# Message tiles of a two-layer graph network: a PSUM ring of eight tiles instead of four, and VectorE's loops written out

## The chip, the cores and the metric

One core of a Trainium2 chip runs the whole program. The metric is the device time of one execution in microseconds (us), lower is better. The engines are TensorE (PE, with its weight loads as PEld), VectorE (DVE), ScalarE (ACT), GpSimd (POOL) and SyncE (SP). PSUM has eight banks of 512 float32 values per partition; a message tile (128 edges by 256 features in float32) takes half a bank.

## The reference

```python
h = jnp.maximum(_layernorm(x), 0.0)                       # x: 3125 x 256
support = h @ L0_weight
msgs = support[src] * edge_weight[:, None]                # 50000 edges
x = x + segment_sum(msgs, dst, 3125) + L0_bias
h = jnp.maximum(_layernorm(x), 0.0)
xt = einsum('ni,rio->rno', h, L1_weight)                  # 8 relations
messages = xt[edge_type, dst]
x = x + relu(segment_sum(messages, src, 3125) + L1_bias)
```

Both layers gather one row of 256 values per edge from a table in DRAM and add it to the row of its target node. Layer 0 adds by `dst`, layer 1 by `src`.

## The kernel before

The edges are taken in four chunks of 25,000: chunks 1 and 2 (`m` = 0, 1) are the halves of layer 0, chunks 3 and 4 (`m` = 2, 3) those of layer 1. Each chunk is sorted by target block of 128 nodes into `T` = 220 tiles of 128 places, in groups of `U` = 20 tiles (eleven groups per chunk). For each tile four engines work in turn:

- POOL issues an indirect gather of 128 rows into a ring in SBUF (L440 in layer 0, ring of 20 tiles, one gather per tile; L456 in layer 1, ring of 32, 196 gathers per chunk). In layer 0 the indices of four gathers at a time are copied by ACT (`refill`, L535) after the message that last used the slots.
- DVE writes the one-hot matrix `oh_m` of the tile's target rows five tiles ahead (`one_hot`, L910, L913).
- PE multiplies it with the gathered rows into half a PSUM bank (`message`, L1304, and `step_message`, L1323).
- DVE adds that half bank to the block's rows four tiles later (`accumulate`, L925), at an offset that it loads into registers four tiles at a time (`offsets`, L917).

Message tiles take turns in banks 2 and 3: a ring of `RING` = 4 tiles. PE may write an even tile `t` only when tile `t` - 3 has been added (a wait on `s_acc`, one per pair of tiles); DVE adds a pair when both of its messages are there (a wait on `s_msg`).

While a chunk's messages run, the next chunk is sorted in the same instruction streams. Every five tiles DVE makes one block of one-hots (`sort_fields`, L848, in layer 0 also L852 and L853), ACT scales it (L502, fifteen instructions per block for the second chunk, ten for the later ones), DVE writes one `oh_t` per tile (L860), and PE runs two to five matmuls per tile (`sort_column`, L1295). In chunks 1 and 2 the chunk after next is ranked too: in groups 0 to 4 PE counts blocks from DVE's masks (L674), group 5 (`chain_side`) is a serial chain between DVE and PE (`rank_chain`; waits at L744, L773), and groups 6 to 9 take places (`take_places`, L707, from PE's matmuls L1243 and L1245). In the last group DVE decodes the sorted index of the next chunk (L868 to L903). During chunk 2 PE also makes layer 1's table (L1440) in banks 4, 5 and 6.

Every engine runs its instructions in the order in which they are written. PE's code is written out tile by tile. DVE's is written out for chunks 2 and 4; for chunks 1 and 3 (`phase`) groups 1 to 4 are one loop (L1017), groups 6 to 9 another (L1021), with addresses and wait values worked out in registers; groups 0, 5 and 10 are written out.

Of the kernel before, what the change touches and what calls it, by code (L numbers as in the profile page):

```python
# [5 lines left out]
def gnn_kernel(nc, x, src, dst, etype, ew, w0, b0, w1, b1, out):  # L6
# [4 lines left out]
    ALU = mybir.AluOpType  # L11
    ACT = mybir.ActivationFunctionType
    ds = bass.ds

    P = 128
    N, D = x.shape
# [11 lines left out]
    NS = 2 * CH  # L28

    T = (EP * CC + (P - 1) * NB) // P  # L30
    U = 20
# [7 lines left out]
    OR = 10  # L39
    RF = 4  # L40
    RING = 4

    BEHIND = (0, 8, 3, 3)
    TU = 5
    SI = CC // U
# [52 lines left out]
    with ctx:  # L98
        def sb(name, shape, dt=f32):
            return ctx.enter_context(nc.sbuf_tensor(name, shape, dt))  # L100
# [3 lines left out]
        def sb_under(name, shape, dt=f32):  # L104
            at[name] = -(-nc.sbuf_base // 32) * 32
            return sb(name, shape, dt)
# [4 lines left out]
        def sem(name):  # L111
            return ctx.enter_context(nc.semaphore(name))
# [47 lines left out]
                      for j, n in enumerate(("hi", "lo")))  # L160
# [50 lines left out]
        rows = sb_under("rows", [P, U, D])  # L211
# [16 lines left out]
        oh_m = sb("oh_m", [P, OR, P])  # L228
        oh_f0 = [sb_over("w1_hi" if k < 3 else "w1_sb", f"oh_f0_{k}", [EP, FR, P, G], f16 if k < 2 else bf16,
                         off=k % 3 * FR * P * G * 2) for k in range(5)]  # L230
# [9 lines left out]
        bank = [ctx.enter_context(nc.psum_tensor(f"bank{i}", [P, 512], f32)) for i in range(8)]  # L240
# [38 lines left out]
        def column(k):  # L279
            return RANK[0:KP, 320 + k:321 + k]  # L280

        def message_bank(u):
            return bank[2 + u // 2 % 2][:, u % 2 * D:(u % 2 + 1) * D]

        s_const = sem("s_const")
        s_ident = sem("s_ident")
# [65 lines left out]
        s_acc = sem("s_acc")  # L352
# [267 lines left out]
        def _(dve):  # L620
# [7 lines left out]
            V = nc.vector  # L628
# [20 lines left out]
            def buckets(s):  # L649
                node = dst_i if s < CH else src_i  # L650
                step(V.tensor_scalar(tmp_i[:, :], chunk(node, s), 7, None, ALU.logical_shift_right))
                step(V.tensor_copy(bucket[:, :], tmp_i[:, :]))
# [191 lines left out]
            def sort_fields(s, c, group, r):  # L844

                places, into = ring_of(s)
                dve.wait_ge(s_sortfree, c + (G + col0(s)))
                V.tensor_tensor(places[:, r, :, :], iota_g16[0:EP, :, :], over_places(pos_p[s % 2], c),  # L848
                                ALU.is_equal).then_inc(s_ohp, 1)
                if s < CH:  # L850
                    dve.wait_ge(s_ohp, group + (col0(s) // G + 1))
                    V.tensor_tensor(into[0][:, r, :, :], places[:, r, :, :], over_places(hi16[s], c), ALU.mult)  # L852
                    V.tensor_tensor(into[1][:, r, :, :], places[:, r, :, :], over_places(lo16[s], c), ALU.mult)  # L853
                if s == 0:
                    V.tensor_tensor(into[2][:, r, :, :], places[:, r, :, :], over_places(ew16[0], c), ALU.mult)
                    if c >= MORE:
                        V.tensor_tensor(into[3][:, r, :, :], places[:, r, :, :], over_places(ew16[1], c), ALU.mult)

            def sort_tile(s, c, slot):
                V.tensor_scalar(oh_t[:, slot, :], iota_t16[0:EP, :], pos_t[s % 2][:, ds(c, 1)], None,  # L860
                                ALU.is_equal).then_inc(s_sortready, 1)
# [46 lines left out]
            def one_hot(s, t, slot):  # L908
                if s < CH:
                    V.tensor_scalar(oh_m[:, slot, :], iota_p[:, :], local[s % 2][:, ds(t, 1)],  # L910
                                    ew_s[s % 2][:, ds(t, 1)], ALU.is_equal, ALU.mult).then_inc(s_ohm, 1)
                else:
                    V.tensor_scalar(oh_m[:, slot, :], iota_p[:, :], local[s % 2][:, ds(t, 1)], None,  # L913
                                    ALU.is_equal).then_inc(s_ohm, 1)

            def offsets(s, t):
                _, got = nc.values_load_multi_w_load_instructions(  # L917
                    tile_off[s % (NS - 1)][0:1, ds(t, LAG)], engines=[mybir.EngineType.DVE], min_val=0,
                    max_val=(NB - 1) * D, skip_runtime_bounds_check_because="tile_offsets() clamps them")
                return got  # L920

            def accumulate(s, off, u, t):
                acc = (x1_sb if s < CH else agg1)[:, :, :].rearrange("p b d -> p (b d)")
                dve.wait_ge(s_acc, t + (s * T + 1))
                V.tensor_tensor(acc[:, ds(off, D)], acc[:, ds(off, D)], message_bank(u), ALU.add).then_inc(s_acc, 1)  # L925

            def message_group(m, i, first=False, last=False, sort=False, side=None, summed=None, after=None):

                for u in range(U):
                    back = (m, i * U + (u - LAG)) if u >= LAG or not first else None  # L930
                    if back is None and m % CH:
                        back = (m - 1, T - LAG + u)
                    if back and u % LAG == 0:
                        got = offsets(*back)
                    if back and u % 2 == 0:
                        dve.wait_ge(s_msg, back[1] + (back[0] * T + 2))
                    if sort:
                        if u % G == 0:
                            sort_fields(m + 1, i * U + u, i * (U // G) + u // G, u // G % FR)
                        sort_tile(m + 1, i * U + u, u % SR)  # L940
                    if side:
                        side(i, u)
                    if u + AH < U or not last:
                        one_hot(m, i * U + (u + AH), (u + AH) % OR)
                    elif m + 1 < NS:
                        one_hot(m + 1, u + AH - U, (u + AH) % OR)
                    if back:
                        accumulate(back[0], got[u % LAG], (u - LAG) % U, back[1])
                        if summed:
                            summed(i * U + (u - LAG + 1))  # L950
                    if after:
                        after(i * U + u)
# [10 lines left out]
            def rank_side(s):  # L963
                def side(i, u):
                    if u % 4 == 1:
                        masks(s, i * TU + u // 4)
                return side
# [43 lines left out]
            def phase(m, ending=None, summed=None):  # L1011
                sort, rank = m + 1 < NS, m + 2 < NS
                if rank:
                    buckets(m + 2)
                side = rank_side(m + 2) if rank else None
                message_group(m, 0, first=True, sort=sort, side=side)
                with dve.Fori(1, TU) as i:  # L1017
                    message_group(m, i, sort=sort, side=side)
                message_group(m, TU, sort=sort, side=chain_side(m + 2) if rank else None)
                side = place_side(m + 2) if rank else None  # L1020
                with dve.Fori(TU + 1, SI) as i:  # L1021
                    message_group(m, i, sort=sort, side=side)
                if ending:
                    ending()
                message_group(m, TI - 1, last=True, side=last_side(m, last_places(m + 2) if rank else None),
                              summed=summed)
# [120 lines left out]
            side = rank_side(CH + 1)  # L1147
# [3 lines left out]
            side = place_side(CH + 1)  # L1151
# [41 lines left out]
        def _(pe):  # L1193
            TE = nc.tensor
# [104 lines left out]
            def message(m, i, u, first):  # L1299
                pe.wait_ge(s_ohm, i * U + (u + 1 + m * T))  # L1300
                pe.wait_ge(s_gather[u], i * 16 + 16 * (1 + m * TI))
                if u % 2 == 0 and not (first and m == 0 and u < RING):
                    pe.wait_ge(s_acc, i * U + (u + 3 - RING + m * T))
                TE.matmul(message_bank(u), oh_m[:, u % OR, :], rows[:, u, :],  # L1304
                          start=True, stop=True).then_inc(s_msg, 1)

            rows1_flat = rows1[:, :, :].rearrange("p r d -> p (r d)")
# [7 lines left out]
            def step_message(m, t, slot):  # L1315
                u = t % U
                pe.wait_ge(s_ohm, t + 1 + m * T)
                if t == 0 or NEED[t] > NEED[t - 1]:
                    g = (m - CH) * TG + NEED[t]
                    pe.wait_ge(s_rows[g % RR], 16 * (g // RR + 1))  # L1320
                if u % 2 == 0:
                    pe.wait_ge(s_acc, t + 3 - RING + m * T)
                TE.matmul(message_bank(u), oh_m[:, u % OR, :], rows1_flat[:, ds(slot, D)],  # L1323
                          start=True, stop=True).then_inc(s_msg, 1)

            def group(m, i, first=False, last=False, sort=False, side=None):
# [133 lines left out]
            for m in range(CH, NS):  # L1460
                pe.wait_ge(s_decoded, m + 1)
                sort = m + 1 < NS
# [30 lines left out]
```

## Time and profile before

| | us |
|---|---|
| median of 3 runs (1303.9 to 1307.88) | 1305.94 |
| the profiled execution, its own time | 1309.25 |
| its span, first to last instruction | 1307.5 |
| busy: PE, DVE, POOL, ACT | 1022.4, 990.9, 908.0, 752.1 |

The messages of chunk 1 run from 165 to 472 us of the span, those of chunk 2 from 472 to 781, the rest of the table to 806, chunk 3 from 806 to 1055 and chunk 4 from 1055 to 1301. No engine is busy over 78% of the span, so the bound has to be read stage by stage. Tiles are numbered through layer 0 from 0: tile 99 is the last before the serial chain of chunk 1, tile 200 the first of its last group, tile 220 the first of chunk 2.

### The profile page before, as it was taken

What the parts mean: (1) busy time and instruction counts of PE and PEld (TensorE: products, weight loads), DVE (VectorE), ACT (ScalarE), POOL (GpSimd) and SP (SyncE); (2) the same over time, 40 slices, a digit from 0 to 9 for tenths busy, and PEclk for the clock granted to TensorE, in tenths of its full rate; (3) what the DMA queues carried; (4) which work ended last, traced back from release to release, by engine and by line L of the source; (5) the groups of instructions that cost most, each with busy time, mean ns of one, the idle gap of its engine ahead of it and who ended that gap; (6) DMA issues with size and microseconds to landing.
All of it is one profiled execution on the core that took longest, in us unless ns stands there. A gap on an engine that the chain in (4) does not pass through costs nothing.

```text
span 1307.5 us, 24085 instructions
## 1 busy us (share of the span) xinstructions
PE 1022.4 (78%) x5311; PEld 732.6 (56%) x5311; DVE 990.9 (76%) x3416; ACT 752.1 (58%) x2039; POOL 908.0 (69%) x921
## 2 busy tenths in 40 slices
PE   5588867786887869998899997777777676776665
PEld 3578746665666647876677775444545432343333
DVE  7899899998888888876787765777777755555554
ACT  4999579995788548887588735767666300000000
POOL 1878577777777677777567623777777777777775
PEclk9999969997999979999999998999899979778887
DMA  4011233333333654666456664333333334444443
GB/s 146 2 31 39 45 101 101 101 99 100 97 97 100 89 158 145 190 198 181 129 182 184 169 132 137 104 104 106 104 105 105 105 112 119 117 117 117 117 121 90
DMA packets 83402, 150.29 MB, mean 115 GB/s; under 512 B 18262, under 2 KB 56628, under 8 KB 83300
## 3 DMA queue, kind: packets, MB, share of 16 engines
q0 software_dynamic: 42400, 109.49, 32.3%
q1 hardware_dynamic: 40900, 39.55, 9.0%
q8 instruction: 50, 0.82, 0.3%
q14 instruction: 52, 0.43, 0.1%
HBM read 115.90 MB, written 32.99 MB: 114 GB/s over the span
## 4 chain that ended last, share of the span: by engine, by line
PE 39%; DVE 19%; POOL 13%; issue 13%; DMA 9%; ACT 4%; DVEq 3%; ACTq 0%; POOLq 0%; SPq 0%
POOL rows L456 13%; PE bank L1304 12%; PE bank L1440 10%; DMA rows<-table,idx 8%; PE bank L1295 7%; PE bank L1323 7%; DVE x_sb L925 4%; DVE oh_t L860 3%; ACT oh_f L502 3%; DVE oh_m L910 2%; DVE oh_p L848 2%; DMA x_sb<-in_x_dram 1%; DVEq L917 1%; DVE oh_f L853 1%; DVE oh_m L913 1%
## 5 line engine op out<-in xcount | busy, mean ns | idle before, releaser
L440 POOL DMA_INDIRECT rows<-table,idx_ring x440 | 436.3, 992 | 172.4 <-issue 123.9
L456 POOL DMA_INDIRECT rows<-table,idx x392 | 373.9, 954 | 160.9 <-issue 143.8
L1323 PE MATMUL bank<-rows,oh_m 128*128 x880 | 333.0, 481 | 139.6 <-DMA rows<-table,idx 69.7
L925 DVE TENSOR_TENSOR x_sb<-x_sb,bank 128x256 f32 x880 | 364.4, 414 | 9.6 <-PE bank L1323 5.6
L1295 PE MATMUL bank<-oh_t,oh_f 125*128 125x220 bf16 x2425 | 352.1, 264 | 14.8 <-DVE oh_t L860 14.1
L1304 PE MATMUL bank<-rows,oh_m 128*128 128x256 f32 x880 | 287.2, 413 | 88.4 <-DVE x_sb L925 87.4
L502 ACT ACTIVATE oh_f<-oh_p,ew_part 125x128 bf16<-125x128 f16 x800 | 307.5, 681 | 32.2 <-DVE oh_p L848 29.5
L1295 PEld LDWEIGHTS bank<-oh_t,oh_f 125*128 125x128 f16 (+1 forms) x2425 | 263.9, 119 | 103.9 <-ACT oh_f L502 17.2
L502 ACT ACTIVATE oh_f<-oh_p,hi 125x128 f16<-125x128 f16 x400 | 269.9, 675 | 74.4 <-DVE oh_p L848 74.4
L1323 PEld LDWEIGHTS bank<-rows,oh_m 128*128 128x128 f32 x880 | 159.5, 219 | 264.9 <-issue 256.6
L860 DVE TENSOR_SCALAR oh_t<-iota_t,pos_t 125x220 bf16<-125x220 f16 x725 | 217.0, 312 | 77.7 <-PE bank L1323 38.7
L502 ACT ACTIVATE oh_f<-oh_p,lo 125x128 f16<-125x128 f16 x400 | 271.4, 679 | 0.0
L1304 PEld LDWEIGHTS bank<-rows,oh_m 128*128 128x128 f32 x880 | 149.8, 200 | 128.6 <-DVE oh_m L910 110.4
L913 DVE TENSOR_SCALAR oh_m<-iota_p,local 128x128 f32<-128x128 f32 x440 | 137.1, 312 | 100.3 <-PE bank L1323 98.2
L910 DVE TENSOR_SCALAR oh_m<-iota_p,local,ew_s 128x128 f32<-128x128 f32 x440 | 158.7, 361 | 7.4 <-PE bank L1304 6.0
L423 POOL DMA_INDIRECT scattered<-pay,place x75 | 93.4, 1246 | 52.8 <-issue 52.5
L848 DVE TENSOR_TENSOR oh_p<-iota_g,pos_p 125x640 f16<-125x640 f16 x145 | 80.2, 553 | 27.6 <-PE bank L1304 11.3
L1440 PE MATMUL bank<-w_hi,hT_hi 128*128 128x512 f32 x200 | 96.5, 483 | 1.5 <-issue 1.5
L535 ACT ACTIVATE idx_ring<-idx 128x4 int32<-128x4 int32 (+1 forms) x110 | 27.3, 253 | 102.1 <-PE bank L1304 88.6
L603 ACT ACTIVATE stage<-bank 128x512 f32<-128x512 f32 x100 | 61.8, 623 | 31.3 <-PE bank L1304 16.5
L1440 PE MATMUL bank<-w_lo,hT_hi 128*128 128x512 f32 x200 | 79.7, 399 | 0.0
L1440 PE MATMUL bank<-w_hi,hT_lo 128*128 128x512 f32 x200 | 79.3, 397 | 0.0
(210 smaller groups left out, 715.5 us busy)
## 6 DMA issues: line engine op xcount, KB each, us to landing
table<-stage SPq DMA_DIRECT2D x100, 256.0 KB, 2.9
rows<-table,idx_ring POOLq DMA_INDIRECT x440, 2.9
rows<-table,idx POOLq DMA_INDIRECT x392, 2.7
table<-stage SPq DMA_DIRECT2D x25, 128.0 KB, 1.8
x_sb<-in_x_dram SPq DMA_DIRECT2D x1, 3072.0 KB
out_dram<-done_first SPq DMA_DIRECT2D x20, 128.0 KB
w_sb<-in_L_gnn_weight_dram SPq DMA_DIRECT2D x2, 1024.0 KB, 12.8
scattered<-pay,place POOLq DMA_INDIRECT x75
```

The source lines that it names most:

```text
L440: pool.indirect_dma_start(out=rows[:, u, :], out_offset=None, in_=table0[:, :], in_offset=bass.IndirectOffsetOnAxis(ap=idx_ring[:, u:u + 1 ...
L456: pool.indirect_dma_start(out=rows1[:, g % RR, :], out_offset=None, in_=table1[:, :], in_offset=bass.IndirectOffsetOnAxis(ap=idx[s % 2][:, ...
L502: last = nc.scalar.activation(into[k][:, r, :, v], places[:, r, :, v], ACT.Copy, scale=f[:, ds(cols + v, 1)])
L848: V.tensor_tensor(places[:, r, :, :], iota_g16[0:EP, :, :], over_places(pos_p[s % 2], c), ALU.is_equal).then_inc(s_ohp, 1)
L860: V.tensor_scalar(oh_t[:, slot, :], iota_t16[0:EP, :], pos_t[s % 2][:, ds(c, 1)], None, ALU.is_equal).then_inc(s_sortready, 1)
L910: V.tensor_scalar(oh_m[:, slot, :], iota_p[:, :], local[s % 2][:, ds(t, 1)], ew_s[s % 2][:, ds(t, 1)], ALU.is_equal, ALU.mult).then_inc(s_ ...
L913: V.tensor_scalar(oh_m[:, slot, :], iota_p[:, :], local[s % 2][:, ds(t, 1)], None, ALU.is_equal).then_inc(s_ohm, 1)
L925: V.tensor_tensor(acc[:, ds(off, D)], acc[:, ds(off, D)], message_bank(u), ALU.add).then_inc(s_acc, 1)
L1295: last = TE.matmul(sorted_field(k), fields[k][:, r, :, v], oh_t[:, slot, :], start=False, stop=False)
L1304: TE.matmul(message_bank(u), oh_m[:, u % OR, :], rows[:, u, :], start=True, stop=True).then_inc(s_msg, 1)
L1323: TE.matmul(message_bank(u), oh_m[:, u % OR, :], rows1_flat[:, ds(slot, D)], start=True, stop=True).then_inc(s_msg, 1)
L1440: last = TE.matmul(table_bank(q)[:, :], h[:, k % HR, j, :], w[:, j, 2 * g:2 * g + 2, :].rearrange("p r d -> p (r d)"), start=(j + v == 0), ...
```

## The change

`message_bank` now takes the chunk and the tile: chunks 1, 3 and 4 rotate through banks 2, 3, 4 and 5 (eight tiles), chunk 2 stays in banks 2 and 3, since 4 to 6 hold its table products. `message_ring` gives the distance that the waits use: 4 in chunk 2 and for the first four tiles of chunk 3, else 8. Because the bank now depends on the tile over more than one turn of a register loop, the two DVE loops of `phase` become Python loops, so that DVE's code for chunks 1 and 3 is written out in full.

```diff
-        def message_bank(u):
-            return bank[2 + u // 2 % 2][:, u % 2 * D:(u % 2 + 1) * D]
+        def message_bank(m, t):
+
+            pair = t // 2 + (T // 2 if m == NS - 1 else 0)
+            return bank[2 + pair % (2 if m == 1 else 4)][:, t % 2 * D:(t % 2 + 1) * D]
+
+        def message_ring(m, t):
+            return RING if m == 1 or m == 2 and t < RING else 2 * RING
...
-                V.tensor_tensor(acc[:, ds(off, D)], acc[:, ds(off, D)], message_bank(u), ALU.add).then_inc(s_acc, 1)
+                V.tensor_tensor(acc[:, ds(off, D)], acc[:, ds(off, D)], message_bank(s, t), ALU.add).then_inc(s_acc, 1)
...
-                message_group(m, 0, first=True, sort=sort, side=side)
-                with dve.Fori(1, TU) as i:
-                    message_group(m, i, sort=sort, side=side)
+                for i in range(TU):
+                    message_group(m, i, first=i == 0, sort=sort, side=side)
...
-                with dve.Fori(TU + 1, SI) as i:
+                for i in range(TU + 1, SI):
                     message_group(m, i, sort=sort, side=side)
...
-                if u % 2 == 0 and not (first and m == 0 and u < RING):
-                    pe.wait_ge(s_acc, i * U + (u + 3 - RING + m * T))
-                TE.matmul(message_bank(u), oh_m[:, u % OR, :], rows[:, u, :],
+                ring = message_ring(m, i * U + u)
+                if u % 2 == 0 and i * U + u + m * T >= ring:
+                    pe.wait_ge(s_acc, i * U + u + 3 - ring + m * T)
+                TE.matmul(message_bank(m, i * U + u), oh_m[:, u % OR, :], rows[:, u, :],
...
-                    pe.wait_ge(s_acc, t + 3 - RING + m * T)
-                TE.matmul(message_bank(u), oh_m[:, u % OR, :], rows1_flat[:, ds(slot, D)],
+                    pe.wait_ge(s_acc, t + 3 - message_ring(m, t) + m * T)
+                TE.matmul(message_bank(m, t), oh_m[:, u % OR, :], rows1_flat[:, ds(slot, D)],
```

PE at the first tiles of chunk 1, before (`s_gather` marks the landed rows, `s_ohm` the one-hot, `s_acc` the added tiles):

```order
L1304 MATMUL bank2<-rows,oh_m 128x256 [waits s_gather0,s_ohm]
L1304 MATMUL bank2<-rows,oh_m 128x256 [waits s_gather1,s_ohm]
L1304 MATMUL bank3<-rows,oh_m 128x256 [waits s_gather2,s_ohm]
L1304 MATMUL bank3<-rows,oh_m 128x256 [waits s_gather3,s_ohm]
L1204 MATMUL bank7<-mask,tape 96x200 [waits s_mask,s_tileoff,s_min]
L1304 MATMUL bank2<-rows,oh_m 128x256 [waits s_acc,s_gather4,s_ohm]
L1304 MATMUL bank2<-rows,oh_m 128x256 [waits s_gather5,s_ohm]
L1304 MATMUL bank3<-rows,oh_m 128x256 [waits s_acc,s_gather6,s_ohm]
```

The same place after (the code lies five lines lower):

```order
L1309 MATMUL bank2<-rows,oh_m 128x256 [waits s_gather0,s_ohm]
L1309 MATMUL bank2<-rows,oh_m 128x256 [waits s_gather1,s_ohm]
L1309 MATMUL bank3<-rows,oh_m 128x256 [waits s_gather2,s_ohm]
L1309 MATMUL bank3<-rows,oh_m 128x256 [waits s_gather3,s_ohm]
L1208 MATMUL bank7<-mask,tape 96x200 [waits s_mask,s_tileoff,s_min]
L1309 MATMUL bank4<-rows,oh_m 128x256 [waits s_gather4,s_ohm]
L1309 MATMUL bank4<-rows,oh_m 128x256 [waits s_gather5,s_ohm]
L1309 MATMUL bank5<-rows,oh_m 128x256 [waits s_gather6,s_ohm]
```

Tiles 4 to 7 lie in banks 4 and 5, and their wait on `s_acc` is gone; later tiles keep it with a value four lower. Nothing else moves on PE, ACT, POOL or SP.

DVE in groups 6 to 9 of chunk 1, from the load of four offsets to the next block of sort one-hots, before (rows of REGISTER_ALU and ISA are the sequencer's register work and waits):

```order
L917 REGISTER_ALU
L917 TENSOR_LOAD tile_off0
L860 ISA [waits s_msg]
L860 TENSOR_SCALAR oh_t<-iota_t16,pos_t1 125x220
L910 ISA
L910 TENSOR_SCALAR oh_m<-iota_p,local0,ew_s0 128x128
L925 ISA [waits s_acc]
L925 TENSOR_TENSOR x1_sb<-x1_sb,bank2 128x256
L847 REGISTER_ALU
L848 ISA [waits s_sortfree]
L848 TENSOR_TENSOR oh_p0_66<-iota_g16,pos_p1 125x640
```

And after:

```order
L922 TENSOR_LOAD tile_off0
L865 TENSOR_SCALAR oh_t<-iota_t16,pos_t1 125x220 [waits s_msg]
L915 TENSOR_SCALAR oh_m<-iota_p,local0,ew_s0 128x128
L930 ISA [waits s_acc]
L930 TENSOR_TENSOR x1_sb<-x1_sb,bank2 128x256
L853 TENSOR_TENSOR oh_p0_66<-iota_g16,pos_p1 125x640 [waits s_sortfree]
```

DVE's work and its order are the same; the register rows of the loop are gone, except the one that holds the accumulator's offset. DVE's program grows from 3659 to 4494 rows.

## Rows read from the trace of the kernel before

**Rows 1.** Busy us and instructions per engine by stage, then granted clock and DMA.

```profile
core 0: us, PE busy (x) PEld busy (x) DVE busy (x) ACT busy (x) POOL busy (x), PEclk, DMA share, GB/s
197.00:298.00 101.00, 79.41 (x580) 66.12 (x580) 92.90 (x310) 91.38 (x262) 77.70 (x77) 1.00 0.35 100
298.00:340.00 42.00, 31.71 (x156) 22.66 (x156) 33.59 (x119) 21.89 (x63) 32.25 (x33) 0.72 0.36 101
340.00:446.00 106.00, 83.29 (x598) 68.33 (x598) 92.57 (x297) 92.58 (x260) 76.78 (x79) 1.00 0.37 97
472.00:643.00 171.00, 154.24 (x798) 118.48 (x799) 137.21 (x514) 130.20 (x350) 123.94 (x125) 0.96 0.55 160
806.00:1055.00 249.00, 185.02 (x849) 118.88 (x850) 185.31 (x694) 155.24 (x400) 188.99 (x198) 0.95 0.37 105
1055.00:1303.00 248.00, 176.82 (x440) 88.76 (x438) 138.18 (x459) 0.00 (x0) 182.91 (x193) 0.80 0.40 115
```

**Rows 2.** Gathers alone: window, its us, POOL's busy us and gathers begun (x).

```profile
161.00:292.30 131.30, 100.43 (x100) 0.92 0.34 99
161.00:427.90 266.90, 200.91 (x201) 0.92 0.35 99
486.20:602.00 115.80, 88.08 (x92) 1.00 0.60 177
...
803.00:1049.50 246.50, 186.74 (x196) 0.95 0.36 104
1050.00:1295.50 245.50, 185.81 (x197) 0.81 0.41 118
```

**Rows 3.** POOL's groups in 197 to 298, 457 to 486.3 and 806 to 1303 us.

```profile
L440 POOL DMA_INDIRECT rows<-table,idx_ring x77 | 78.3, 1017 | 23.5 <-issue 22.2 <-ACT idx_ring L535 1.2
...
L440 POOL DMA_INDIRECT rows<-table,idx_ring x21 | 23.6, 1125 | 9.4 <-issue 5.8 <-ACT idx_ring L535 3.6
...
L456 POOL DMA_INDIRECT rows<-table,idx x390 | 372.0, 954 | 118.8 <-issue 101.7 <-PE bank L1323 17.1
```

**Rows 4.** DMA issues of the page: layer 0's gathers, count, median us to landing.

```profile
rows<-table,idx_ring POOLq DMA_INDIRECT x440, 2.9
```

**Rows 5.** Timeline: gather and message of tile 99, message 100; tile 200; tile 260.

```profile
292.29 0.95 POOL L440 DMA_INDIRECT rows<-table,idx_ring  x1 [0.30 <-issue]
...
295.15 0.67 PE L1304 MATMUL bank<-rows,oh_m 128*128 128x256 f32 x2
...
298.41 0.67 PE L1304 MATMUL bank<-rows,oh_m 128*128 128x256 f32 x2 [2.03 <-DVE x_sb L925]
...
427.87 0.95 POOL L440 DMA_INDIRECT rows<-table,idx_ring  x1 [0.30 <-issue]
...
445.95 0.61 PE L1304 MATMUL bank<-rows,oh_m 128*128 128x256 f32 x2
...
511.39 0.95 POOL L440 DMA_INDIRECT rows<-table,idx_ring  x1 [0.30 <-issue]
...
521.22 0.62 PE L1304 MATMUL bank<-rows,oh_m 128*128 128x256 f32 x2
```

**Rows 6.** DVE's waits in 298 to 340 us: total us, times, longest.

```profile
DVE key_row L744 <- PE bank L1215: 2.2, 1, 2.2
DVE tile_off L773 <- PE bank L1258: 1.6, 1, 1.6
DVE oh_t L860 <- PE bank L1304: 1.5, 1, 1.5
DVE oh_p L848 <- PE bank L1304: 1.2, 1, 1.2
```

**Rows 7.** DVE's two longest waits in 340 to 446 us.

```profile
DVE pos_acc L707 <- PE bank L1245: 5.6, 8, 0.9
DVE oh_t L860 <- PE bank L1304: 3.7, 12, 0.3
```

**Rows 8.** PE's waits for the accumulation in layer 1, 806 to 1303 us.

```profile
PE bank L1323 <- DVE x_sb L925: 16.2, 25, 1.1
```

## The prediction

> **What bounds the kernel now.** I read the busy table by stage first, then the gathers alone, then the timeline at three tiles, then DVE's waits.
>
> In layer 1 the gathers set the pace. 196 of them take 246.5 us in chunk 3 and 197 take 245.5 us in chunk 4 [rows 2], 1.258 and 1.246 us each, and every gap between two of them is the engine's own issue gap or a wait that ends with it: 118.8 us of idle time over 390 gathers is 0.30 us each [rows 3], the same 0.30 us that stands before an undisturbed gather [rows 5]. A gather of 0.95 us and a gap of 0.30 make 1.25 us, so POOL has nothing to wait for. PE and DVE are busy about three quarters of that time or less [rows 1].
>
> In layer 0 the bound changes inside a chunk. In the first hundred tiles of chunk 1 DVE (92.9 of 101 us) and ACT (91.4) are nearly full [rows 1], yet POOL is the slower one: a gather there takes 1017 ns and its gap 0.305 us [rows 3], 1.32 us each, while the messages go at 1.26 us per tile (101 us for some 80 tiles). It had a head start that is used up just at the end: tile 99's gather starts at 292.29 and lands 2.9 us later [rows 4], at 295.2; its message starts at 295.15 [rows 5]. Message 100 then waits for DVE [rows 5], which has begun the serial chain of group 5. From 298 to 340 us that chain holds everything (42 us for 20 tiles, TensorE at a granted clock of 0.72 [rows 1]), and POOL fills its ring meanwhile. From 340 to 446 us, 80 tiles of 1.325 us, DVE and ACT are busy 92.6 us each [rows 1] and POOL waits for free slots. Chunk 2 is PE's: 154 of 171 us [rows 1].
>
> **The change part by part.**
>
> *Ring, chunk 1, tiles 0 to 99: nothing.* PE runs ahead of DVE, but message 99 already starts when its rows land [rows 4, 5]. Bounds: 0 and -1 us. The loop written out makes DVE faster here, and it waits for gathers instead.
>
> *Ring, chunk 1, the chain (298 to 340 us): -6.5 us.* With four tiles PE may start tile 104 only after DVE has added tile 101, and behind message 104 in PE's queue stands the small matmul that the chain needs (L1215). So DVE arrives at L744 and waits 2.2 us; L773 1.6, L860 1.5 and L848 1.2 are of the same kind, DVE waiting for a PE that it holds up itself [rows 6]. With eight tiles message 104 needs tile 97 added, which DVE has done before the chain's long steps. All four waits go: 2.2 + 1.6 + 1.5 + 1.2 = 6.5. Cover: PE must get its tiles done while DVE works on the chain; DVE's own serial steps stay. Bounds: -3 (the two waits on L744 and L773 keep a matmul's latency) and -6.5.
>
> *Ring and written-out loop, tiles 120 to 199 (340 to 446 us): -9 us.* DVE idles 106 - 92.6 = 13.4 us [rows 1]. L707 waits 5.6 us for place matmuls that stand behind messages held by the ring, and L860 3.7 us at the pairs [rows 7], twelve times 0.3 us, each behind a register load of the loop. The remaining 4.1 us are before the sort blocks; part of it is DVE's wait for its own result and stays. So 9.3 us are named and 13.4 are the end. ACT is as full as DVE (92.58 us), so it gives the same end: 80 tiles cannot take less than 92.6 us. I take 9, the named waits, because three coupled queues with equal loads do not pack without gaps. Bounds: -5 (only L707 goes) and -13.
>
> *Last group of chunk 1 and the way into chunk 2: a cap.* A faster PE empties the gather ring sooner, and POOL's pace becomes the limit. From tile 99 on, 101 gathers at 1.32 us put tile 200's gather at 292.3 + 133 = 425.6 (now 427.87) and its landing at 428.5; its message is now at 445.95 [rows 5], so it can come 17.4 us sooner at most. Then 20 gathers at 1.26 (the pace of 486 to 602 us, 115.8/92 [rows 2]) bring chunk 2's first to 450.8, 20 at 1.40 (1125 ns and 0.28 us of issue [rows 3], slowed by DVE's decoding) to 478.8, and 20 at 1.26 bring tile 260's to 504, against 511.39 now [rows 5]: 7.4 us sooner. Tile 260's rows now land at 514.3 and its message starts at 521.22 [rows 4, 5], a lead of 6.9 us. So the shift at tile 260 is at most 7.4 + 6.9 = 14.3 us. Behind it PE is the slower one again (chunk 2's ring is unchanged), and the shift is handed on as it is.
>
> *Layer 1: nothing.* The larger ring takes away PE's 16.2 us of waits for the accumulation [rows 8], but PE then waits for gathers. POOL's two chunks take 492 us for 393 gathers; at 1.25 us each that is 491. Bounds: -2 and +2 us. The loop written out in chunk 3 frees DVE, which is not the bound.
>
> A rule speaks for more here. The Trainium skill, "Perfetto Trace Analysis", section "Matmul Optimizations", asks that all eight PSUM banks be used for parallelism. By it the 16.2 us would be the gain of layer 1 on top; [rows 2, 3] give 0 to 2.
>
> *Sum.* -6.5 - 9 = -15.5, capped at 14.3. Both are ends without slack, so I take -13. The profiled execution took 1309.25 us (span 1307.5); 1309.25 - 13 = 1296.3. It was 3.3 us above the median of the runs, 1305.94; against that median the forecast is 1305.94 - 13 = **1293 us**.
>
> **The rivals.**
>
> *The gathers eat half of it.* If the gathers of chunk 2 do not start earlier (index decoding comes later than I think, or POOL gets slower beside a busier DVE), the shift ends at tile 260's lead, 6.9 us: 1299. For it: gathers beside sort blocks take 1017 ns instead of layer 1's 954, beside decoding 1125 [rows 3], so DVE's work does slow POOL. Against it: the number of those DVE instructions per gather does not change. The Trainium skill, "SBUF — State Buffer", section "Who interferes with whom", says that a VectorE instruction in a two-port mode locks GpSimd out for its whole length. By that rule a denser DVE costs POOL the same total per tile, and the 0.06 us more per gather is that total.
>
> *The waits only move.* If DVE's gaps in chunk 1 are the sort columns' and not the messages', PE's ring doesn't help, and of the 15.5 us under 3.9 remain: 1303 to 1306. Against it: the releaser of three of the four waits in [rows 6] and one in [rows 7] is named, and they stand behind messages.
>
> *Layer 1 gains too:* 1293 - 16 = 1277, if PE's waits there were on the path. POOL's row [rows 3] is against it.
>
> *Slower.* In chunk 3 a PE that is no longer paced by pairs could run in bursts, idle until rows land, and be granted the lower of its two clocks (1.2 instead of 2.4 GHz) more often. It is busy 185 of 249 us at a mean of 0.95 [rows 1]; at 0.72, the mean of the chain, that is 244 us, still enough. Below 0.71 it decides: at 0.65 it is 270 us, 21 us more, 1293 + 21 = 1314. Against it: chunk 4 has 0.80 with as much idle time [rows 1], and chunk 3 hardly changes its load.
>
> **How the numbers follow.** Under 0.3%, 3.9 us, a measurement of this kernel can't tell a change from none. Forecast (8 to 18 us gained) 0.70; gathers eat half 0.15; waits only move 0.08; layer 1 too 0.03; slower 0.04. Faster is 0.70 + 0.15 + 0.03 = 0.88, same 0.08, slower 0.04. The range goes from 1286 (the cap of 17.4 us at tile 200, and 2 us in layer 1) to 1301 (the first rival with 2 us to spare).
>
> **What would show it.** In the changed profile: tile 99's message still at about 295 us; L744's and L773's waits gone and the chain some 35 us long instead of 42, at a higher granted clock; tiles 120 to 199 in 93 to 99 us; POOL's waits for ACT in chunk 1 gone; chunk 2's first messages waiting for gathers; its table unchanged in length; 246 us each for chunks 3 and 4. The forecast is wrong if DVE's idle share from 340 to 446 us stays, or if chunk 2 grows by what chunk 1 gives.

## The result and the profile after

The changed kernel takes 1301.45 us (median of 12 runs, 1299.56 to 1303.43) against 1306.88 us of the kernel before (12 runs beside it): a ratio of 0.9955, 95% interval 0.9943 to 0.9968. It is faster by 5.4 us. The sign was forecast, but 13 us had been forecast, and the measured time lies just beyond 1301, the slow end of the range. The profiled execution has a span of 1299.6 us, 7.9 us under the 1307.5 us of before. The kernel before had been profiled in an execution of 1309.25 us, 2.4 us above its median, so shifts read from the two profiles are some 2 us larger than the gain in the runs.

Where the messages of a tile start, in us of the two profiled executions (tiles 0 to 219 are chunk 1, 220 to 439 chunk 2, 440 to 659 chunk 3, 660 to 879 chunk 4):

| tile | before | after | shift |
|---|---|---|---|
| 0 | 164.8 | 164.4 | -0.4 |
| 100, the chain begins | 298.4 | 295.4 | -3.0 |
| 120, the chain is over | 340.0 | 324.3 | -15.7 |
| 200, last group of chunk 1 | 446.0 | 424.0 | -22.0 |
| 219, last of chunk 1 | 469.8 | 459.1 | -10.7 |
| 260 | 521.2 | 510.4 | -10.8 |
| 440, chunk 3 begins | 806.2 | 795.3 | -10.9 |
| 660, chunk 4 begins | 1054.6 | 1047.6 | -7.0 |
| 879, last | 1300.0 | 1292.3 | -7.7 |

Half of what chunk 1 gained was lost again inside its last twenty tiles, and four more us in chunk 3. The busy table by stage, cut at the same tiles as [rows 1] (us, busy us and instructions of each engine, granted clock, DMA share, GB/s):

```profile
core 0: us, PE busy (x) PEld busy (x) DVE busy (x) ACT busy (x) POOL busy (x), PEclk, DMA share, GB/s
197.00:295.00 98.00, 84.14 (x551) 63.47 (x550) 89.45 (x300) 86.33 (x253) 75.10 (x76) 1.00 0.37 103
295.00:324.30 29.30, 24.40 (x157) 18.59 (x158) 28.11 (x103) 20.62 (x59) 22.29 (x24) 0.94 0.36 103
324.30:424.00 99.70, 86.15 (x599) 68.50 (x598) 96.33 (x316) 92.56 (x267) 76.13 (x78) 1.00 0.37 103
424.00:460.40 36.40, 21.34 (x88) 12.66 (x87) 21.10 (x69) 0.83 (x6) 27.61 (x29) 0.70 0.78 158
460.40:620.00 159.60, 144.52 (x743) 111.43 (x742) 129.02 (x480) 128.04 (x342) 119.45 (x120) 0.95 0.56 166
792.00:1042.00 250.00, 181.77 (x840) 114.46 (x840) 186.58 (x686) 157.49 (x401) 190.18 (x196) 0.97 0.36 103
1042.50:1295.00 252.50, 188.77 (x448) 100.27 (x446) 139.15 (x466) 0.00 (x0) 186.73 (x196) 0.74 0.40 115
```

The second and third rows are the gain. From 295 to 424 us DVE is busy 28.11 + 96.33 of 129 us and idles 4.6 us; before it idled (42 - 33.59) + (106 - 92.57) = 21.8 us in the 148 us of the same tiles [rows 1]. The fourth row is the loss: for twenty tiles (36.4 us) no engine is busy more than 27.6 us, and the DMA engines are at 0.78.

The timeline at the tiles that matter (start, us, engine, line, and in brackets the wait ahead of it and what ended it):

```profile
292.90 0.67 PE L1309 MATMUL bank<-rows,oh_m 128*128 128x256 f32 x2
...
420.44 0.95 POOL L445 DMA_INDIRECT rows<-table,idx_ring  x1 [0.30 <-issue]
...
423.96 0.61 PE L1309 MATMUL bank<-rows,oh_m 128*128 128x256 f32 x2
...
442.61 1.19 PE L1309 MATMUL bank<-rows,oh_m 128*128 128x256 f32 x2 [3.68 <-DMA rows<-table,idx_ring]
...
444.19 0.95 POOL L445 DMA_INDIRECT rows<-table,idx_ring  x1 [0.30 <-ACT idx_ring L540]
...
459.05 1.19 PE L1309 MATMUL bank<-rows,oh_m 128*128 128x256 f32 x2 [0.21 <-DMA rows<-table,idx_ring]
```

Tile 99 starts at 292.90. Tile 200's gather is issued at 420.44 and its message starts 3.5 us later: the lead of 18 us that it had before [rows 5] is gone. Tile 219's gather is issued at 444.19 and its message starts at 459.05. Fifteen us from issue to use, where the median landing takes 2.9 us [rows 4], is the thing to explain. PE's waits in 424 to 460.3 us (total us, times, longest) name it:

```profile
PE bank L1309 <- DMA rows<-table,idx_ring: 8.7, 7, 3.7
PE bank L1309 <- DVE oh_m L915: 4.0, 3, 2.0
```

and in the kernel before, at the same tiles (446 to 470.5 us), PE waits for no landing at all:

```profile
PE bank L1304 <- DVE x_sb L925: 6.9, 4, 2.9
```

### The profile page after: what moved, and what is told of

Same layout as the page of the kernel before. It is cut to its first block, busy times and chain, and to the rows that moved or that the text cites. A ratio compares the mean times of both kernels' runs of the same rounds, so it can differ in the third digit from the quotient of the medians.

```text
span 1299.6 us, 22920 instructions
## 1 busy us (share of the span) xinstructions
PE 1038.8 (80%) x5311; PEld 737.0 (57%) x5311; DVE 987.4 (76%) x3415; ACT 747.8 (58%) x2039; POOL 908.8 (70%) x921
## 4 chain that ended last, share of the span: by engine, by line
PE 31%; POOL 23%; issue 14%; DMA 13%; DVE 11%; ACT 7%; ACTq 1%; DVEq 0%; POOLq 0%; SPq 0%
POOL rows L461 15%; PE bank L1445 11%; POOL rows L445 9%; DMA rows<-table,idx 9%; PE bank L1309 7%; PE bank L1328 7%; ACT oh_f L507 5%; PE bank L1299 4%; DMA rows<-table,idx_ring 3%; DVE oh_t L865 2%; DVE x_sb L930 2%; DMA x_sb<-in_x_dram 1%; DVE oh_m L915 1%; DVE oh_p L853 1%; DVE oh_f L858 1%
## 5 line engine op out<-in xcount | busy, mean ns | idle before, releaser
L1328 PE MATMUL bank<-rows,oh_m 128*128 x880 | 340.5, 493 | 133.6 <-DMA rows<-table,idx 63.9
L1299 PE MATMUL bank<-oh_t,oh_f 125*128 125x220 bf16 x2425 | 345.7, 261 | 16.5 <-DVE oh_t L865 14.7
L1309 PE MATMUL bank<-rows,oh_m 128*128 128x256 f32 x880 | 289.7, 413 | 66.1 <-DVE x_sb L930 24.4
L1299 PEld LDWEIGHTS bank<-oh_t,oh_f 125*128 125x128 f16 (+1 forms) x2425 | 261.0, 118 | 99.9 <-ACT oh_f L507 18.6
L1328 PEld LDWEIGHTS bank<-rows,oh_m 128*128 128x128 f32 x880 | 167.5, 227 | 262.6 <-issue 251.9
L1309 PEld LDWEIGHTS bank<-rows,oh_m 128*128 128x128 f32 x880 | 147.3, 197 | 120.2 <-DVE oh_m L915 62.6
```

The source lines that it names most:

```text
L1299: last = TE.matmul(sorted_field(k), fields[k][:, r, :, v], oh_t[:, slot, :], start=False, stop=False)
L1309: TE.matmul(message_bank(m, i * U + u), oh_m[:, u % OR, :], rows[:, u, :], start=True, stop=True).then_inc(s_msg, 1)
L1328: TE.matmul(message_bank(m, t), oh_m[:, u % OR, :], rows1_flat[:, ds(slot, D)], start=True, stop=True).then_inc(s_msg, 1)
```

## The experiments

All kernels compute the full result. Times are medians of runs beside the kernel before on the same chip, with the ratio and its 95% interval; the message times are of the profiled executions.

**Which part brings the gain: the written-out loops or the ring?** First the loops alone: written out as in the change, with the ring left at four tiles.

```diff
-            return bank[2 + pair % (2 if m == 1 else 4)][:, t % 2 * D:(t % 2 + 1) * D]
+            return bank[2 + pair % 2][:, t % 2 * D:(t % 2 + 1) * D]
...
-            return RING if m == 1 or m == 2 and t < RING else 2 * RING
+            return RING
```

> Only DVE's two loops are written out; the ring stays at four tiles everywhere. If the ring is what shortens chunk 1's serial chain, tiles 100 to 120 take 41 us here as before (29 in the changed kernel), and only tiles 120 to 200 gain, some 6 us of the 106; at tile 219 nothing is given back, since the gathers still have a lead of some 10 us. If writing out is the whole effect, tile 200 comes 22 us early as in the changed kernel. Chunk 3: the theory that written-out DVE code meets the gathers in a worse phase expects 1.27 to 1.28 us per gather (before 1.262); the theory that the larger ring does it expects 1.262. Total: 1301 to 1304 by the first pair, about 1301 by the second.

Measured: 1302.3 against 1307.63 us (0.9969, 0.9958 to 0.9979). The chain (tiles 100 to 120) takes 39.4 us, tiles 120 to 199 102.8, tile 200 is 8.4 us earlier than before and tile 219 8.8: nothing is given back. DVE's waits in 295 to 335 us and in 334.7 to 437.5 us:

```profile
DVE key_row L749 <- PE bank L1219: 2.4, 1, 2.4
DVE tile_off L778 <- PE bank L1262: 1.6, 1, 1.6
DVE oh_t L865 <- PE bank L1309: 0.4, 1, 0.4
DVE oh_p L853 <- PE bank L1309: 0.2, 1, 0.2
...
DVE pos_acc L712 <- PE bank L1249: 5.3, 8, 0.7
DVE oh_t L865 <- PE bank L1309: 2.7, 12, 0.2
```

The two waits on the chain's small matmuls and the one on the place matmuls are those of [rows 6, 7], nearly unchanged, and the twelve at the pairs fell only from 3.7 to 2.7 us. DVE is as busy as before in both stages (33.2 and 93.1 us). Over the two stages 21.8 us of idle time became (39.4 - 33.2) + (102.8 - 93.1) = 15.9. Of these 5.9 us the two smaller waits of the chain give 2.1 (1.5 + 1.2 became 0.4 + 0.2) and the pairs 1.0; the rest is idle time that these waits don't name.

Then the ring alone: eight tiles, with DVE's loops kept, two groups to a turn so that a bank is known in the code.

```diff
...
-                for i in range(TU):
-                    message_group(m, i, first=i == 0, sort=sort, side=side)
+                message_group(m, 0, first=True, sort=sort, side=side)
+                with dve.Fori(0, TU // 2) as j:
+                    for k in (1, 2):
+                        message_group(m, j * 2 + k, sort=sort, side=side, k=k)
...
```

> The ring of eight tiles as in the changed kernel, but DVE's loops stay loops (of two groups per turn, so that the bank is the same in each turn). Ring theory: tiles 100 to 120 take 29 us, tiles 120 to 200 about 100, tile 200 is 15 to 18 us early. The gathers have some lead left, so less than 11 us is given back up to tile 219, and chunk 2 starts 9 to 11 us early as in the changed kernel. Writing-out theory: chunk 1 as before, total 1306. Chunk 3: 1.262 us per gather if the written-out code slowed it, 1.277 if the ring did.

Measured: 1296.92 against 1307.63 us (0.993, 0.9916 to 0.9945). Stage table, chain and tiles 120 to 199:

```profile
core 0: us, PE busy (x) PEld busy (x) DVE busy (x) ACT busy (x) POOL busy (x), PEclk, DMA share, GB/s
...
292.70:322.90 30.20, 24.89 (x161) 18.68 (x160) 28.52 (x105) 21.50 (x61) 22.89 (x25) 0.94 0.36 103
322.90:421.20 98.30, 83.66 (x599) 68.17 (x597) 94.83 (x311) 91.98 (x265) 74.83 (x78) 1.00 0.37 103
```

Tile 200 comes 24.8 us earlier than before, against 22.0 in the changed kernel, so the ring alone brings all of chunk 1's gain; the 8.4 us of writing out do not come on top, since both end at the gathers. The loss is here too: tile 219 starts at 457.1, 12.7 us earlier than before. Against the changed kernel this version is 4.5 us faster in medians; the two ratios' intervals just touch. The Trainium skill, "Runtime: NRT & Kernel Launch", section "Instruction fetch mechanics", says that a taken branch whose target is not at hand stalls the fetching of instructions, and that this is one reason why kernels prefer full unrolling where possible. Here unrolled code by itself helped (0.9969), but beside the ring it brought nothing, and no row here shows a stall of the fetching.

**What holds chunk 1's last tiles? First theory: the weights.** In the changed kernel layer 1's weights (2 MB in two transfers) are issued at 434.0 us, among these gathers. One kernel holds them back until all messages of chunk 1 have started.

```diff
             sp.wait_ge(s_sorted, CH)
+            sp.wait_ge(s_msg, T)
             for k in range(KC):
```

> The changed kernel, but the load of layer 1's weights (2 MB) is issued only after all 220 messages of chunk 1. Theory that this load takes the DMA engines from gathers without lead: gathers of tiles 208 to 219 land within 3 to 4 us of their start, tile 219's message starts at 447 to 451 us (459.1 in the changed kernel, 469.8 before), and then PE and ACT wait for the weights, so that chunk 2 starts at 466 to 470 and the total is 1305 to 1309. Rival, that DVE's decoding and the lower clock of TensorE hold the last group: tile 219 stays at 457 to 460.

Measured: tile 219 at 454.8 us, between the two theories (a single run, 1305.36 us, in which PE then waits for the weights themselves). Two rows of the stage table and two of the timeline:

```profile
core 0: us, PE busy (x) PEld busy (x) DVE busy (x) ACT busy (x) POOL busy (x), PEclk, DMA share, GB/s
360.00:425.00 65.00, 55.81 (x378) 44.09 (x376) 61.32 (x201) 58.85 (x172) 49.47 (x52) 0.97 0.37 102
425.00:455.00 30.00, 21.07 (x86) 12.24 (x85) 20.79 (x68) 0.71 (x5) 22.99 (x24) 0.74 0.71 96
...
454.85 1.19 PE L1310 MATMUL bank<-rows,oh_m 128*128 128x256 f32 x2 [0.53 <-DMA rows<-table,idx_ring]
...
466.04 0.53 PE L1290 MATMUL bank<-zeros 125*128 125x440 bf16 x1 [10.01 <-DMA w_sb<-in_L_gnn_weight_dram]
```

Without the weights the last gathers still land late, and the DMA engines are 0.71 busy while they move no more than 96 GB/s. In the 65 us before, the same kernel's DMA engines moved 102 GB/s at 0.37. The next kernel spreads the load, 16 pieces over tiles 207 to 230, with the weights' splits moved back to tiles 15 to 20 of chunk 2:

```diff
-            for k in range(KC):
-                sp.dma_start(w1_sb[:, k, :, :],
-                             w1[:, k * P:(k + 1) * P, :].rearrange("r p d -> p r d")).then_inc(s_w, 16)
+            for q in range(KC * R):
+                k, r = divmod(q, R)
+                sp.wait_ge(s_msg, T - 12 + 3 * q // 2)
+                sp.dma_start(w1_sb[:, k, r, :], w1[r, k * P:(k + 1) * P, :]).then_inc(s_w, 16)
...
-            pe.wait_ge(s_w, 16 * (1 + KC))
```

> The changed kernel, but the weights come in 16 pieces of 128 KB, one after every one or two messages from tile 207 to tile 230; PE's wait for them at the start of chunk 2 is dropped, and ACT's and DVE's splitting of them moves to tiles 15 to 20 of chunk 2, before the first table product at tile 26. Load theory: tile 219 at 450 to 454, chunk 2 keeps 15 to 18 us of the 22 gained at tile 200, total 1294 to 1297. Rival (decoding and clock): tile 219 stays at 459, total 1301. A third way: the pieces only shift the collision into chunk 2, tile 260 stays at 510, total 1301.

Measured: 1299.73 against 1307.63 us (0.9948, 0.9934 to 0.9963), tile 219 at 458.1 and tile 260 at 510.7, as in the changed kernel. Counted from tile 200, whose start differs by up to 2.4 us between these kernels, the last twenty tiles take 35.1 us in the changed kernel, 31.8 with the weights spread and 29.6 with the weights held back; it was 23.9 before. So the weights' load has some 5 us in it, but it is not the whole cause, and the theory falls.

**Second theory: the empty tiles.** With the reference's inputs the edges of chunk 1 fill 208 of its 220 tiles. The last twelve are gathered all the same, and every empty place has index 0 (the decoding clamps at 0), so the 128 rows of such a gather are one and the same row of the table. The transfers of the gathers' queue in 440 to 460 us of the kernel before, where these gathers lie (packets, MB, share of 16 engines' time; then the issues):

```profile
q0 software_dynamic: 553, 1.54, 85.5%
...
rows<-table,idx_ring POOLq DMA_INDIRECT x14, 4.9
```

553 packets take 0.855 x 16 x 20 us, which is 0.495 us each. In 360 to 425 us it is 0.16 us each (2327 packets, 35.6% of 16 x 65 us). So the empty gathers were slow before as well, but their issue was 15 us and more ahead of the messages and nobody waited. The test gives every empty place the number of its partition as index, 128 different rows; the rows' contents do not reach the result, since their one-hots are zero.

```diff
-                    V.tensor_scalar(idx[q][:, :], dec_j, -float(KEY_LOW), 0.0, ALU.add, ALU.max).then_inc(s_index, 1)
+                    step(V.tensor_scalar(idx[q][:, :], dec_j, 0.0, part[:, 0:1], ALU.is_equal, ALU.mult))
+                    V.scalar_tensor_tensor(idx[q][:, :], dec_j, -float(KEY_LOW), idx[q][:, :], ALU.add, ALU.max).then_inc(s_index, 1)
```

It was put into the changed kernel, into the version with the ring in loops, into the kernel before as a control, and, with the spread weights, into the ring in loops once more.

> The changed kernel, and the empty places of layer 0's tiles gather 128 different rows of the table (row p for partition p) where they all gather row 0 now. In both kernels the packets of 4 KB that are read in chunk 1's last tiles take 0.72 to 0.78 us on average instead of 0.22; tiles 208 to 219 are the empty ones. Theory (empty tiles read one row, land slowly, and the lead that hid it is gone): packets stay at 0.2 to 0.35 us, the messages of tiles 212 to 219 come at 1.3 us per tile instead of 2.1, tile 219 starts at 449 to 453 instead of 459.1, chunk 2 at 451 to 456; the total is 1294 to 1298. Rival (the weights' load takes the DMA engines): tile 219 stays at 457 to 459, total 1301.

> The ring of eight tiles with DVE's loops kept, and distinct rows for the empty places. If the two add up: tile 219 at 447 to 451 (457.1 with the loops alone), chunk 2 starts 18 to 22 us before the kernel before, gathers of chunk 3 at 1.262 to 1.266 us, total 1289 to 1292. If the weights' load is the limit: total 1297 as with the loops alone.

> The kernel before with distinct rows for the empty places. The theory says that a lead of 15 us hides the slow gathers there: no change, total within 1 us of the kernel before, tile 219 at 469 to 470. If the slow gathers cost something by themselves (they load the DMA engines and HBM beside the weights), it gains 2 to 5 us.

> As the kernel with the ring, the loops and distinct rows, and the weights in 16 pieces from tile 207 on. If the weights' load still delays gathers once the empty tiles are quick, this gains 2 to 5 us on that kernel (total 1285 to 1290); if not, it is the same within 1 us.

| kernel | median us | kernel before | ratio, 95% | tile 200 | tile 219 | tile 260 |
|---|---|---|---|---|---|---|
| changed, distinct rows | 1295.06 | 1307.24 | 0.9917, 0.9903 to 0.9932 | 423.1 | 447.5 | 505.3 |
| ring in loops, distinct rows | 1293.24 | 1307.24 | 0.990, 0.9885 to 0.9916 | 424.1 | 445.9 | 502.6 |
| before, distinct rows | 1309.62 | 1307.24 | 1.002, 1.0008 to 1.0031 | 445.5 | 469.7 | 521.7 |
| ring in loops, distinct rows, weights spread | 1293.77 | 1307.24 | 0.9906, 0.9887 to 0.9924 | 425.8 | 447.4 | 505.9 |

With distinct rows the twenty last tiles of the changed kernel take 24.4 us; it was 35.1 with one row and 23.9 before. The rival named with the first theory, that DVE's decoding and TensorE's lower clock hold the last group, falls with it: the decoding is still there, one instruction longer, and the kernel before took its 23.9 us at a granted clock of 0.79. The control gains nothing, so the edit is worth time only where PE has caught up with the gathers. Its tile 219 comes at 469.7 as expected, but in the runs it is 2.4 us slower, where 1 us had been allowed; that stays open. The ring in loops gains 3.7 us from distinct rows (1296.92 to 1293.24, on two chips) and not the 5 to 8 that were expected, though its tile 219 comes 11 us earlier: further on its messages wait for chunk 2's gathers (below). The queue's row of 440 to 460 us in the control, which has as many such packets there as the kernel before:

```profile
q0 software_dynamic: 576, 1.57, 28.1%
```

and of the changed kernel with distinct rows:

```profile
q0 software_dynamic: 819, 2.24, 35.5%
```

0.156 and 0.139 us a packet, against 0.495 in the kernel before and, in the changed kernel, whose window holds some of chunk 2's gathers too, 0.278:

```profile
q0 software_dynamic: 857, 2.36, 74.4%
```

The last twelve gathers of chunk 2 (428 to 439) are of the same kind. The queue's row of 740 to 770 us in the kernel before and in the control, 0.395 and 0.163 us a packet:

```profile
q0 software_dynamic: 757, 2.05, 62.3%
...
q0 software_dynamic: 705, 1.91, 23.9%
```

There the gathers lead the messages by 19 us before and after, and nothing is lost.

The weights travel in chunk 1's last stage too, and once the rows differ it makes no difference in the runs whether they are spread (1293.77 against 1293.24). Beside the slow gathers they cost some 5 us (29.6 against 35.1), beside quick ones spreading them brings nothing that shows. That settles the 11 us. Why one row that a whole gather shares is read slowly no run here shows; nor was another row than row 0 tried.

Not all of it reaches chunk 3. With distinct rows the changed kernel is 22.3 us ahead of the kernel before at tile 219 and 15.9 at tile 260. Between them PE now waits for chunk 2's gathers (its waits in 455 to 506 us), and around tile 240 a message starts 2.8 us after its gather:

```profile
PE bank L1310 <- DMA rows<-table,idx_ring: 3.2, 7, 0.8
```

**Chunk 3.** From its first gather to chunk 4's first, chunk 3 takes 247.3 us before and 250.4 us after. The changed kernel was run once more for that. It and the two versions with distinct rows were also run with chunk 3 as before (ring of four, loops); part of the edit:

```diff
-            return bank[2 + pair % (2 if m == 1 else 4)][:, t % 2 * D:(t % 2 + 1) * D]
+            return bank[2 + pair % (2 if m in (1, 2) else 4)][:, t % 2 * D:(t % 2 + 1) * D]
...
-            return RING if m == 1 or m == 2 and t < RING else 2 * RING
+            return RING if m in (1, 2) else 2 * RING
...
+                if m == CH:
+                    with dve.Fori(1, TU) as i:
+                        message_group(m, i, sort=sort, side=side, k=1)
```

> The changed kernel unaltered, on the same chip as the next three, to see how far one profile of chunk 3 differs from another: from the first gather of chunk 3 to the first of chunk 4 it took 250.4 us (247.3 before). If that is a property of the code, 249.5 to 251 again; if it varies with the run, anything from 247 to 251. Total 1299 to 1302, tile 219 at 458 to 460.

> The changed kernel with chunk 3 as it was before (DVE's loops, ring of four tiles); chunks 1 and 4 as changed. Theory that the change itself slows chunk 3's gathers through DVE's timing: chunk 3 takes 247 to 247.5 us, total 2 to 3 us below the changed kernel on this chip. If chunk 3's time varies with the run: no difference beyond 1 us.

> Ring of eight tiles in chunks 1 and 4, DVE's loops kept, chunk 3 as before, distinct rows for the empty places. Theory: 1 us below the kernel with ring, loops and distinct rows (1293), if chunk 3 takes 247 instead of 248.1 us: 1291 to 1293. If chunk 3 does not care: 1293.

> The changed kernel with distinct rows for the empty places and chunk 3 as before (chunk 1 written out). Tile 219 at 446 to 449, tile 260 at 503 to 506, chunk 3 in 247 to 248 us, total 1292 to 1295. Against the best kernel above it tells whether writing out chunk 1 costs anything once the empty tiles are quick: theory says no, since gathers set the pace there, difference within 2 us.

The kernel before took 1307.3 us beside these four.

| kernel | median us | ratio, 95% | chunk 3, us |
|---|---|---|---|
| changed, again | 1302.22 | 0.9953, 0.9938 to 0.9968 | 250.6 |
| changed, chunk 3 as before | 1300.76 | 0.994, 0.9925 to 0.9955 | 248.0 |
| ring in loops, distinct rows, chunk 3 as before | 1294.63 | 0.9898, 0.9883 to 0.9913 | 248.3 |
| changed, distinct rows, chunk 3 as before | 1293.94 | 0.9891, 0.9876 to 0.9907 | 247.5 |

POOL's row for these 196 gathers (total us, mean ns of one; idle time and its ends), in the changed kernel:

```profile
L461 POOL DMA_INDIRECT rows<-table,idx x196 | 190.6, 973 | 101.2 <-issue 90.5 <-PE bank L1328 10.7
```

and with chunk 3 as before:

```profile
L461 POOL DMA_INDIRECT rows<-table,idx x196 | 188.2, 960 | 101.5 <-issue 49.4 <-DMA table<-stage 42.1 <-PE bank L1337 10.1
```

The idle time is the same; the gathers themselves are longer, 973 ns against 960 (957 in the kernel before). Over eight profiles chunk 3 takes 246.7 to 248.3 us in the code of before or with the ring in loops, and 248.2 to 250.6 in five profiles of the changed code. That is about 2 us, but the lowest of the five, 248.2 with gathers of 962 ns, is the changed kernel with distinct rows, whose chunk 3 has the same code. What it is worth in the runs, 1.5 us between the first two rows of the table where 2 to 3 had been expected, lies inside their intervals, so an effect of chunk 3's code is likely and not shown. With distinct rows, putting chunk 3 back changed nothing that the intervals tell apart. The ring in loops, 248.1 in three profiles, says that the ring alone isn't it; the written-out loop with a ring of four took 249.3, which points at the loop, on one profile.

The five versions with distinct rows and the larger ring lie between 1293.2 and 1295.1 us, about 1% under the kernel before. The runs don't tell them apart.

## Why the prediction was right in sign and wrong in size

*Ring, tiles 0 to 99, nothing: too low by little.* Tile 99 starts 2.2 us earlier (bounds 0 and -1), because the gathers that it waits for came faster.

*The chain, -6.5, and tiles 120 to 199, -9: the mechanism and the sum were right.* L744's and L773's waits are gone, the granted clock in the chain rose from 0.72 to 0.94, and DVE's idle time fell by 17.3 us over both stages (7.2 in the chain, 10.0 behind it) where 15.5 had been named. By tiles it looks different: the chain gave 12.7 us and tiles 120 to 199 gave 6.3, since some DVE work that stood in the chain now stands behind it (119 instructions before and 103 after in the one stage, 297 and 316 in the other). One detail was wrong: the 3.7 us at the pairs were put down to a register load of the loop, but 2.7 of them stayed when the loop was written out alone, and they are gone with the ring.

*The cap of 17.4 us at tile 200: a cap, but mis-sized.* The message of tile 200 does end up waiting for its gather, as forecast. But the gather itself came 7.4 us earlier, not 2.3. The size that failed is the gather's: 1.32 us each rests on 1017 ns beside sort work, with a gap of 0.305 us [rows 3]. The gap held. The gather did not; POOL's row in 197 to 295 us of the changed kernel, and the gathers alone from 161 us to tile 200's:

```profile
L445 POOL DMA_INDIRECT rows<-table,idx_ring x76 | 75.1, 988 | 23.1 <-issue 21.6 <-ACT idx_ring L540 1.5
...
161.00:420.50 259.50, 198.17 (x201) 0.97 0.36 102
```

Tile 99's gather starts 2.2 us earlier than before, and the 101 gathers behind it take 1.29 us each, not 1.32: together the 5.2 us by which tile 200's gather beats the forecast 425.6. Against the kernel before, 201 gathers take 986 ns each instead of 1000, and 0.305 us of idle time each instead of 0.328 [rows 2]. So 22.0 us could be gained by tile 200, and were. Why the gathers became shorter is not shown. DVE is as busy beside them as before (89.45 of 98 us, 92.90 of 101 [rows 1]), so the rival's argument, that the same DVE work costs POOL the same per gather, does not hold here. In 197 to 295 us they take 977 ns with the loops alone written out and 980 with the ring in loops, and 1016 again in the control.

*The way into chunk 2: the step that failed.* The text let 20 gathers follow at 1.26 us and land in 2.9 us, and let PE take them as they come. Their issue went as priced (1.25 us each). It is their landing that failed, which was taken from a median over 440 gathers. The last twelve of chunk 1 are another kind: all their 128 places read one row. In the kernel before, the lead of the gathers hid it; the very gain of chunk 1 used that lead up. This term was missing, and it is +11.3 us at tile 219. The prediction's own sign of being wrong, that chunk 2 grows by what chunk 1 gives, came some tiles early. With distinct rows the cap at tile 260 is seen at work: PE waits for gathers on the way to it, and the shift is 15.9 us, with the ring in loops 18.6, where 14.3 had been put as the most. Then the gain in the runs is 12.2 us against a forecast of 13. That the two lie so near is in part luck, since the cap was too low and layer 1 gives some back. The row from which the slow landing could have been seen was in the trace of before: 0.94 of the DMA engines' time for 77 GB/s.

```profile
425.00:446.00 21.00, 17.00 (x126) 14.05 (x125) 18.55 (x61) 17.68 (x51) 15.03 (x16) 1.00 0.45 93
446.00:460.00 14.00, 10.34 (x71) 8.10 (x69) 10.78 (x35) 0.51 (x3) 8.30 (x10) 0.99 0.94 77
```

*Chunk 2 hands the shift on, and its table is unchanged: right.* The shift is 10.7 us at tile 219, 10.8 at 260, 10.9 at 440.

*Layer 1, nothing (-2 to +2): too narrow.* PE's waits for the accumulation fell from 16.2 us [rows 8] to 3.3, and the gain from that is nil, as forecast: the way from message 440 to message 879 took 493.8 us before and 497.0 after. POOL's gathers set it (392 of them in the two chunks; the prediction's 393 counts one in both windows), and PE's longest waits are for their rows:

```profile
PE bank L1328 <- DMA rows<-table,idx: 63.9, 110, 2.4
...
PE bank L1328 <- DVE x_sb L930: 3.3, 4, 0.9
```

The 3.2 us more are chunk 3's longer gathers. The Trainium skill's rule to use all eight banks ("Perfetto Trace Analysis", "Matmul Optimizations") gave nothing in layer 1; the 16 us that the prediction worked out by it are not in the trace.

*The rivals.* The measured time of 1301.45 is near the 1299 of "the gathers eat half of it", but not for its reason: chunk 2's gathers start 12 us earlier, not as late as before, and it is their predecessors' landing that held. "Slower" by a low clock in chunk 3 did not come (0.97).

## What to carry to other kernels

When a change lets a consumer catch up with its producer, the landing of each transfer must be read at the very place where they will meet, not from a median over all of them; a stretch with a high DMA share and few GB/s is a slow transfer that only a lead hides. Padding that points all at one place is work that a gather pays for: give empty places distinct rows. And a cap that is built on an instruction's length beside other work (here 1017 ns for a gather) holds only as long as that work stays where it is: after the change it was 988.

## What the runs showed of the hardware

Gathers whose 128 rows are one row of the table land slowly: 0.50 us a packet (mean over the queue's packets in that window) against 0.16, and 85.5% of the DMA engines' time where distinct rows took 28.1% for about as many bytes. And a gather's own length on POOL differs between kernels that change only DVE's loops and the ring: in 197 to 298 us of chunk 1 1017 ns before and 1016 in the control, 977 to 997 in 197 to 295 us of all changed kernels; in chunk 3 962 to 974 with DVE's loop written out and the larger ring, 954 to 961 with the loop. The cause of this stays open.
